# Low-rank products of the gate and up weights moved to the start of a two-layer kernel and added by accumulating transfers

## What is computed

```python
gate = einsum('btd,edf->ebtf', x, Wg);  up = einsum('btd,edf->ebtf', x, Wu)     # 8 experts, 256 x 256
gate = gate.at[:2].add(einsum('btd,edr,erf->ebtf', x, Ga, Gb))                  # rank 64
up   = up.at[:2].add(einsum('btd,edr,erf->ebtf', x, Ua, Ub))
mid  = silu(gate) * up
out  = einsum('ebtf,efd->ebtd', mid, Wd);  out = out.at[:2].add(... Da, Db)     # rank 64
return einsum('bte,ebtd->btd', weights, out)
```

## Time and profile before

| | |
|---|---|
| median of 3 runs | 437.26 us (437.18 to 437.58) |
| the profiled execution | 437.48 us |
| its span | 435.7 us |
| TensorE busy | 424.1 us, 97% of the span |
| VectorE busy | 347.3 us, 80% |
| ScalarE, GpSimd busy | 177.9 us (41%), 170.7 us (39%) |
| mean granted TensorE clock | 0.995 |

### The profile page before, as it was taken

The page is one execution under the profiler, slowest core; times in us unless marked ns, Lnnn a source line. Parts: engine busy times, 40 slices in busy tenths (PEclk is TensorE's granted clock), DMA queues, the critical chain, the costliest instruction groups (busy, mean ns, idle before and its releaser), DMA issues.

```text
span 435.7 us, 7495 instructions
## 1 busy us (share of the span) xinstructions
PE 424.1 (97%) x2520; PEld 369.7 (85%) x2520; DVE 347.3 (80%) x1090; ACT 177.9 (41%) x333; POOL 170.7 (39%) x201
## 2 busy tenths in 40 slices
PE   7999999999999999999999999999999999999993
PEld 5788888987888998878888989789889888999883
DVE  6787899998899668889994898899977566667882
ACT  5445445423262826342446234423552253525030
POOL 2416479351026202500064707010720064727387
PEclk9999999999999999999999999999999999999997
DMA  8992499990002130000021300000203613512375
GB/s 287 300 415 76 137 251 269 267 247 20 2 12 86 50 97 2 0 2 1 2 97 35 112 2 0 2 0 2 79 20 95 196 49 122 183 50 93 131 244 174
DMA packets 33382, 45.84 MB, mean 105 GB/s; under 512 B 2696, under 2 KB 29600, under 8 KB 32704
## 3 DMA queue, kind: packets, MB, share of 16 engines
q1 hardware_dynamic: 29712, 37.32, 29.5%
q0 software_dynamic: 2640, 7.22, 4.7%
q10 hardware_dynamic: 992, 0.81, 0.6%
HBM read 22.22 MB, written 23.13 MB: 104 GB/s over the span
## 4 chain that ended last, share of the span: by engine, by line
PE 85%; POOL 5%; issue 3%; DMA 2%; DVE 2%; ACT 1%; POOLq 0%; SPq 0%; DVEq 0%
PE D L687 25%; PE G L687 23%; PE U L687 23%; PE M L687 8%; POOL returned L619 2%; POOL fetched L625 2%; PE M L696 1%; PE D L716 1%; DMA fetched<-returned 1%; PE M L813 1%; DMA rows<-x 1%; PE M L838 1%; PE M L708 1%; DMA returned<-made_down,w_raw 1%; DVE w_lo L1343 1%
## 5 line engine op out<-in xcount | busy, mean ns | idle before, releaser
L687 PE MATMUL D<-w_hi,mid_hi 128*128 128x256 f32 x264 | 75.4, 286 | 0.0
L687 PE MATMUL D<-w_hi,mid_lo 128*128 128x256 f32 x264 | 74.7, 283 | 0.0
L687 PE MATMUL D<-w_lo,mid_hi 128*128 128x256 f32 x264 | 74.7, 283 | 0.0
L1091 ACT ACTIVATE mid<-G 128x512 f32<-128x512 f32 x64 | 37.9, 596 | 76.4 <-PE G L687 66.1
L1464 DVE TENSOR_TENSOR mid<-mid,U 128x512 f32<-128x512 f32 x64 | 43.3, 685 | 26.0 <-PE U L687 13.2
L530 POOL TENSOR_TENSOR w_lo<-w_raw,w_hi 128x512 fp32r<-128x512 f32 x35 | 46.9, 1371 | 27.2 <-ACT w_hi L1064 18.7
L1478 DVE SCALAR_TENSOR_TENSOR rows<-D,weight,rows 128x256 f32<-128x256 f32 x128 | 54.0, 476 | 4.4 <-PE D L687 4.1
L1064 ACT ACTIVATE mid_hi<-mid 128x512 fp32r<-128x512 f32 x64 | 39.9, 630 | 37.4 <-DVE mid L1464 37.2
L1343 DVE TENSOR_TENSOR mid_lo<-mid,mid_hi 128x512 fp32r<-128x512 f32 x64 | 48.3, 774 | 6.1 <-ACT mid_hi L1064 4.6
L687 PEld LDWEIGHTS D<-w_hi,mid_hi 128*128 128x128 f32 x264 | 50.5, 191 | 1.7 <-issue 1.0
L687 PEld LDWEIGHTS D<-w_lo,mid_hi 128*128 128x128 f32 x264 | 50.6, 192 | 0.7
(11 more groups left out here) (355 smaller groups left out, 955.2 us busy)
## 6 DMA issues: line engine op xcount, KB each, us to landing
sorted_rows<-weighted SPq DMA_DIRECT2D x8, 1542.0 KB, 21.2
w_raw<-weights SPq DMA_DIRECT2D x5, 1024.0 KB, 18.2
stage<-sorted_rows SPq DMA_DIRECT2D x31, 128.5 KB, 2.2
fetched<-returned SPq DMA_DIRECT2D x6, 512.0 KB, 6.5
w_raw<-weights SPq DMA_DIRECT2D x3, 768.0 KB, 11.4
rows<-x SPq DMA_DIRECT2D x7, 256.0 KB, 3.2
w_raw<-weights SPq DMA_DIRECT2D x4, 256.0 KB, 5.6
w_raw<-weights SPq DMA_DIRECT2D x2, 512.0 KB, 7.3
```

The source lines that it names most:

```text
L687: ins = nc.tensor.matmul(out_ap, a, b, start=(first and n == 0), stop=(last and n == 3 * len(pairs) - 1))
L1091: nc.scalar.activation(mid[:, c, :], GU[2 * c][:, :], ACT.Silu).then_inc(silu_ready, 1)
```

## The change

The products for gate0, up0, gate1 and up1 (the first four, `LORA_HELD`) are made at the very start, behind 12 warming products in place of 20, into banks G1, U1, D0 and D1. ScalarE copies each into its weight's place in `w_raw` (`hold_lora`). The raw gate and up weights of experts 0 and 1 are no longer loaded by SyncE: GpSimd issues one transfer for each expert that adds them to what lies there (`accum_op=ALU.add`). The two products for down0 and down1 stay at e = 4, VectorE's additions for them at e = 5. The factors of gate and up are loaded ahead of all weights. ScalarE's `high(2)` goes behind `x_high(0)`.

```diff
--- before.py
+++ after.py
@@ -64,8 +64,10 @@
 
 LORA_NAMES = ("gate0", "up0", "gate1", "up1", "down0", "down1")
 
-CHUNKS = ((0, 1), (1, 2), (2, 4), (4, 5), (5, 8), (8, 10), (10, 13), (13, 17), (17, 21), (21, 25), (25, 28),
-          (28, 32), (32, 36), (36, 37))
+LORA_HELD = 4
+JOINED = tuple((WHERE[f"gate{_e}"], WHERE[f"gate{_e}"] + 2) for _e in range(2))
+CHUNKS = ((0, 1), (1, 2), (2, 4), (4, 5), (5, 8), (8, 10), (10, 13), (13, JOINED[0][0]), JOINED[0],
+          (JOINED[0][1], JOINED[1][0]), JOINED[1], (JOINED[1][1], 28), (28, 32), (32, 36), (36, 37))
 CHUNK_OF = {n: c for c, (first, end) in enumerate(CHUNKS) for n in range(first, end)}
 assert sorted(CHUNK_OF) == list(range(MATS))
 
@@ -74,7 +76,7 @@
 VECTOR_LOW = (0, 1)
 POOL_LOW = tuple(n for n in range(MATS) if n not in VECTOR_LOW)
 FIRST_BETA = 3
-WARMUPS = 20
+WARMUPS = 12
 SMALL = 2 * KC * E + 2 * SCANS + 1 + 3 * KC
 
 
@@ -243,7 +245,7 @@
         GU = [G0, U0, G1, U1]
         DN = [D0, D1]
         MT = [M0, M1]
-        LORA_PS = [M0, M1, M0, M1, M0, M1]
+        LORA_PS = [G1, U1, D0, D1, M0, M1]
         LORA_FACTORS = [(gu_factors, 0), (gu_factors, 0), (gu_factors, RANK), (gu_factors, RANK),
                         (down_factors, 0), (down_factors, 0)]
 
@@ -270,6 +272,7 @@
         toep_made = sem("toep_made")
         powers_made = sem("powers_made")
         lora_ps = sem("lora_ps")
+        lora_held = sem("lora_held")
         lora_added = sem("lora_added")
         high_ready = sem("high_ready")
         vector_low_ready = sem("vector_low_ready")
@@ -428,18 +431,19 @@
                 sp.dma_start(gu_factors[rows, :, :], lora_gu[rows, :, :]).then_inc(lora_gu_loaded[e], 16)
 
             load_x(sp, 0, 0)
+            load_gu(0)
+            load_gu(1)
             for c in range(6):
                 load_chunk(c)
             sp.dma_start(beta[:, :], beta_row[:, :].partition_broadcast(P)).then_inc(beta_loaded, 16)
-            load_gu(0)
             load_chunk(6)
-            load_gu(1)
             sp.dma_start(down_factors[:, :, :], lora_down[:, :, :]).then_inc(lora_down_loaded, 16)
             sp.wait_ge(bias_made, 1)
             for row in BIAS_ROWS:
                 sp.dma_start(bias_raw[row:row + E, :], bias[:, :]).then_inc(bias_loaded, 16)
             for c in range(7, len(CHUNKS)):
-                load_chunk(c)
+                if CHUNKS[c] not in JOINED:
+                    load_chunk(c)
             sp.wait_ge(xn_ready, 2)
             for half in range(2):
                 load_x(sp, 1, half)
@@ -535,6 +539,11 @@
             split_low(2, 4)
             pool.wait_ge(powers_made, 1)
             split_low(4, 7)
+            for e in range(2):
+                first, end = JOINED[e]
+                pool.wait_ge(lora_held, 2 * (e + 1))
+                nc.gpsimd.dma_start(w_raw[:, first:end, :], weights[:, first:end, :], accum_op=ALU.add)\
+                    .then_inc(chunk_loaded[CHUNK_OF[first]], 16)
             pool.wait_ge(mid_ready, at(0, 2 * E, 2 * 1 + 2))
             split_low(7, 8)
             pool.wait_ge(routed, 1)
@@ -924,10 +933,15 @@
 
             pe.wait_ge(warm_made, 1)
             for _ in range(WARMUPS):
-                nc.tensor.matmul(D1[:, :], xT_lo[:, 0, 0:P], xT_lo[:, 0, :], start=True, stop=True)
+                nc.tensor.matmul(M0[:, :], xT_lo[:, 0, 0:P], xT_lo[:, 0, :], start=True, stop=True)
+            for i in range(LORA_HELD):
+                if i % 2 == 0:
+                    pe.wait_ge(lora_gu_loaded[i // 2], 16)
+                lora(i)
             pe.wait_ge(const_made, 5)
             transpose_x(0)
             first_gate_up()
+            pe.wait_ge(lora_held, 2)
             gate_up(0, 0, [1])
             pe.wait_ge(routers_ready, 1)
             router_start(M0, 0, xT_hi, xT_lo, (logitT_ps[0], 1))
@@ -962,23 +976,14 @@
                         unit(1, owners)
                     if e == SCAN_AT[g] + 1:
                         scan(g)
-                    if g == 0 and e == 2:
-                        pe.wait_ge(logit0_ready, 1)
-                        pe.wait_ge(lora_gu_loaded[0], 16)
-                        for i in (0, 1):
-                            lora(i)
-                    if g == 0 and e == 3:
-                        pe.wait_ge(lora_added, 2)
-                        pe.wait_ge(lora_gu_loaded[1], 16)
-                        for i in (2, 3):
-                            lora(i)
-                    if g == 0 and e == 4:
-                        pe.wait_ge(lora_added, 4)
-                        pe.wait_ge(lora_down_loaded, 16)
-                        for i in (4, 5):
-                            lora(i)
+                    if g == 0 and e == 1:
+                        pe.wait_ge(lora_held, LORA_HELD)
                     if e == 1:
                         pe.wait_ge(logit0_ready, at(g, 1, 1))
+                    if g == 0 and e == 4:
+                        pe.wait_ge(lora_down_loaded, 16)
+                        for i in range(LORA_HELD, LORA):
+                            lora(i)
                     if g and e == 3:
                         moments(g - 1, 0)
                     if g and e == 5:
@@ -991,7 +996,7 @@
                     if g and e == 4:
                         transpose_gates(g - 1)
                     if e == SCAN_AT[g]:
-                        pe.wait_ge(lora_added, LORA)
+                        pe.wait_ge(lora_added, LORA - LORA_HELD)
                         if g:
                             pe.wait_ge(result_ready, at(g - 1, TILES, TILES))
                         scan_input(g)
@@ -1068,11 +1073,15 @@
 
             def high(n):
 
-                if NAMES[n] in LORA_NAMES:
-                    act.wait_ge(lora_added, LORA_NAMES.index(NAMES[n]) + 1)
+                if NAMES[n] in LORA_NAMES[LORA_HELD:]:
+                    act.wait_ge(lora_added, LORA_NAMES.index(NAMES[n]) - LORA_HELD + 1)
                 else:
                     act.wait_ge(chunk_loaded[CHUNK_OF[n]], 16)
                 copy(w_hi[:, n, :, :].rearrange("p k d -> p (k d)"), w_raw[:, n, :]).then_inc(high_ready, 1)
+
+            def hold_lora(i):
+                act.wait_ge(lora_ps, i + 1)
+                copy(w_raw[:, WHERE[LORA_NAMES[i]], :], LORA_PS[i][:, :]).then_inc(lora_held, 1)
 
             def x_high(g):
                 for k in range(KC):
@@ -1129,14 +1138,18 @@
             nc.scalar.activation(lam[:, 0, :], lam[:, 0, :], ACT.Tanh, scale=0.5).then_inc(lam_tanh, 1)
             nc.scalar.activation(decay, decay, ACT.Tanh, scale=0.5).then_inc(decay_tanh, 1)
             high(0)
+            x_norm(0)
             high(1)
-            x_norm(0)
+            x_high(0)
             high(2)
-            x_high(0)
             high(3)
+            hold_lora(0)
             silu(0, 0, 0, mid_used=False)
+            hold_lora(1)
             high(4)
             high(5)
+            hold_lora(2)
+            hold_lora(3)
             silu(0, 0, 1, mid_used=False)
             high(6)
             logits_out(0, 0)
@@ -1769,9 +1782,9 @@
                         mid_mul(g, e, [0])
                         if late:
                             unit_low(0)
-                        if first and e in (3, 4, 5):
-                            add_lora(2 * e - 6)
-                            add_lora(2 * e - 5)
+                        if first and e == 5:
+                            for i in range(LORA_HELD, LORA):
+                                add_lora(i)
                         if first and e == NORM_AT[g]:
                             stats = x_stats(nxt)
                         if g and e == 2:
```

## The result

The changed kernel is slower: 439.02 us median of 6 runs (438.78 to 439.5), beside 437.22 (437.12 to 437.58, 6 runs) for the kernel before, ratio 1.0042 (95% interval 1.0029 to 1.0055). The forecast was 436.6, at most 438.3. A later job gave 439.73 beside 437.26, ratio 1.0058 (1.0041 to 1.0075).

What follows compares the result with a forecast made beforehand. TensorE, busy 97% of the span, was taken as the bound, with VectorE deciding where gains pass. The terms - 2.01 - 0.09 + 0.77 + 0.70 = - 0.63 gave 436.6 us against the median, range 435.3 to 438.3.

Steps and rivals of the forecast that it cites:

- The pair at e = 3: TensorE at e = 3: without the low-rank pair the down product follows at once and VectorE keeps up; minus 2.01 us.
- The pair at e = 2: TensorE at e = 2: down product still waits for VectorE's additions, so 1.92 us become a stall; minus 0.09 us.
- The start: Opening: two pairs of factor products behind twelve warming products delay the transposes and ScalarE's copy of xT; plus 0.77 us.
- The collision: Opening: GpSimd's consecutive splits hold up VectorE's tiny instruction and `mid_lo`, so the router starts late; plus 0.70 us.
- Rival 4: Opening: TensorE waits for late factors, slower from a landing at 9.35, 442.5 us at the old transfer time; chance 0.14.
- Rivals 1 and 2: Collision costs the router nothing, 435.9 us, chance 0.22; both pairs pay in full, 434.0 us, chance 0.05.
- rival 3: Rest eaten by another lost turn between GpSimd and VectorE or slightly late factors; 437.2 to 438.0 us, chance 0.17.
- Hidden: ScalarE's four product copies, 0.55 us each, and GpSimd's accumulating transfers, first read about 45.4, were to cost nothing.

Runs made afterwards that it cites:

- busy_e3: Changed kernel with nine zero products ahead of the down product at e = 3, giving back 2.0 us of TensorE; 439.57 us, ratio 1.0050 to the kernel before.
- one_pair: Kernel before with only the products of gate1 and up1 put first, the pair of gate0 and up0 left at e = 2; ratio 1.0007.
- fill: Changed kernel with ten zero products filling TensorE's stall at e = 2 of group 0; ratio 1.0019 to the kernel before.
- fill_again: First repeat of the changed kernel with ten zero products in the stall at e = 2; 448.78 us, ratio 1.0003 to the kernel before.
- fill_c: Second repeat, on a quiet chip, of the changed kernel with ten zero products in the stall at e = 2; 438.51 us, ratio 1.0028.
- pool_before: Kernel before with GpSimd's splits of matrices 14 to 19 put ahead of its addition of beta in group 0; ratio 1.0162.
- act_back: Changed kernel with ScalarE's opening copies back in their old order; 438.24 us, ratio 1.0028 to the kernel before.
- pool_after: Changed kernel with GpSimd's splits of matrices 14 to 19 put ahead of its addition of beta in group 0; ratio 1.0006 to the kernel before.

## Why the prediction was wrong

The forecast was 0.63 us less than the profiled time, and the result is 1.88 more at the landmark. By its steps:

- **The pair at e = 3, minus 2.01.** TensorE gained it: up at 44.70, down at 44.92. The step that failed is the sentence behind it, "in the full stretch that follows it comes forward with TensorE". VectorE did come forward, but only to the chained steps at 59.6, and those end when GpSimd's splits end. The splits hang on beta, and beta on the additions at e = 2, which stand ahead of anything that this pair could free. Worth: 0.2 (busy_e3), 0.19 (one_pair). Those steps, 0.35 and 1.21 where the others took 0.16 (they run beside the end of the splits), stood in the trace of before and I didn't read them.
- **The pair at e = 2, minus 0.09, and the rest a stall.** Right as far as it went: a stall of 2.38, released by the additions. What was missing is its price. "The pair filled a wait that VectorE makes anyway" was half of what it did; it also kept TensorE's clock up. Plus 1.50 where the clock falls (fill, fill_again, fill_c: 75.60 to 74.1), in no term and no rival.
- **The start, plus 0.77.** The mechanism was right and the size wrong. The first copy of xT came 0.14 later (9.78 for 9.64), and in the changed kernel's three profiles the last up record of e = 2 stood at 32.27 to 32.37 for 32.07: 0.2 to 0.3. The pairs overlap (2.90 us for 3.93), which no row of before could show. But the 5.84 at which the factors were to begin also took it for granted that the clock comes up at 4.7, as in the one trace read; it varies. With the 0.74 of idle time gone, nothing takes up a late start any more. Over thirteen profiles with both pairs first, the last up record stood between 32.18 and 33.21, so this term was 0.1 to 1.1. With the opening of before, pool_before's warming products stood 0.43 apart until 6 us and its record was at 31.85 all the same.
- **The collision, plus 0.70.** Right at the router (0.76 with the opening's 0.14 in it), and 0.73 at the down product of e = 2. At the landmark little of it is separate: what remains of the 1.88 beside the clock (1.50) and the opening (0.20) is 0.18. The parts found elsewhere add up to that: 0.52 for the collision (act_back), less 0.20 to 0.30 for the pair at e = 3 (busy_e3; one_pair, 73.62 for 73.92).
- **Rival 4, slower by late factors.** The right sign for the wrong reason: in the changed kernel's profile TensorE waited for no factors, though they landed later than forecast (5.9 and 7.0 for 5.4 and 6.8) and so just in time. In one profile, pool_after, they were late (6.75 for the first) and it waited some 0.6. Rivals 1 and 2 failed with the stall; rival 3 had the turns between GpSimd and VectorE but no place where they matter.
- Hidden, as forecast: the four copies on ScalarE (the silu at 12.44 and 16.05), and the accumulating transfers, issued at 21.45 and 22.23 and landed 11.9 us later in the median, well ahead of their reader at 46.45.

The Trainium skill ("TensorE: Matmul & The Clock Gate", in its part on the clock gate) says that an idle array goes back to 1.2 GHz. The profiles agree that it does, 0.66 of the full clock in 35 to 40 us. Its "SBUF — State Buffer" ("Who interferes with whom") names the shared pair of ports for VectorE and GpSimd, and the steps of 1.2 beside splits agree.

## What to carry to other kernels

Before work is moved out of a wait, ask what it did there beside its own result: here it kept TensorE busy, and its removal cost 1.5 us in each profiled execution in which the clock then fell. Idle time can also take up the spread of what comes before it: once it is used up, that spread reaches the end. One profiled execution shows one cause; the clock and the times of all executions tell how often it is there. A microsecond won on the engine that is busy 97% is worth nothing if a later rendezvous is set by another chain; follow the gain forward, on every engine, to the next place where all of them meet, and look there for short steps that take ten times their usual time. Where two engines take turns, moving one engine's batch moves the loss; measure such a move at a landmark behind the whole stretch, not at the place that it clears.
